# A state-space scan on one Trainium2 core: delta and delta*u spread over the states by DMA instead of by matmul

## The reference, cut to what matters

```python
u = silu(xc + conv_b)
dt, Bm, Cm = split(einsum('gld,ed->gle', u, x_proj_w), [1, 17])
delta = softplus(einsum('glr,dr->gld', dt, dt_proj_w) + dt_proj_b)
A = -exp(A_log)
def step(h, inputs):
    d_t, u_t, B_t, C_t = inputs
    dA = exp(d_t[..., None] * A)
    h = h * dA + (d_t * u_t)[..., None] * B_t[:, None, :]
    return h, einsum('gdn,gn->gd', h, C_t)
y = (ys + u * D) * silu(z)
```

## Time and profile before

| | us |
|---|---|
| median of 3 runs | 10411.63 (10410.5 to 10415.53) |
| the profiled execution, as timed | 10411.98 |
| its span | 10410.2 |
| of it the Mamba stage, first `drive` to last gate | 709.89 to 8072.94 |
| mean granted clock of TensorE, share of full speed | 0.878 |

### The profile page before, as it was taken

How to read it: one execution, slowest core, us unless ns; L and a number is a source line. 1 busy time by engine, 2 the same in 40 slices (tenths; PEclk the granted TensorE clock), 3 DMA queues, 4 the chain that set the end, 5 groups by cost and what they waited for, 6 DMA issues and landing times. The chain is left out here.

```text
span 10410.2 us, 140735 instructions
## 1 busy us (share of the span) xinstructions
PE 8332.9 (80%) x34187; PEld 4314.8 (41%) x34187; DVE 7595.6 (73%) x10036; ACT 5478.6 (53%) x9098; POOL 5384.7 (52%) x4490
## 2 busy tenths in 40 slices
PE   9977777777777777777777777777777899999997
PEld 9942222222222222222222222222222599977996
DVE  7769898898989898898989889898988112211222
ACT  0346666666666666666666666666666013311332
POOL 0027677777777777676777777677777000000000
PEclk9978888878888888888888788888888999999998
DMA  9631111111111111111111111111111100030002
GB/s 175 170 80 33 32 35 30 38 28 35 32 32 35 29 36 28 38 29 35 33 31 36 28 36 31 33 32 32 35 30 36 56 10 0 0 75 19 0 0 49
DMA packets 644678, 403.37 MB, mean 39 GB/s; under 512 B 399312, under 2 KB 631120, under 8 KB 643664
## 3 DMA queue, kind: packets, MB, share of 16 engines
q1 hardware_dynamic: 407888, 318.19, 12.2%
q10 hardware_dynamic: 236032, 77.08, 3.2%
HBM read 136.43 MB, written 103.80 MB: 23 GB/s over the span
## 5 line engine op out<-in xcount | busy, mean ns | idle before, releaser
L636 POOL TENSOR_TENSOR prod<-hs,bsp 128x448 f32<-128x448 f32 x3584 | 4378.9, 1248 | 1489.7 <-PE ps L647 800.0
L624 DVE TENSOR_TENSOR_SCAN hs<-da,hs,ps 128x448 f32<-128x448 f32 x3072 | 3482.8, 1134 | 1.5
L605 ACT ACTIVATE da<-ps,nega 128x448 f32<-128x448 f32 x3586 | 2215.2, 634 | 1746.5 <-PE ps L588 1698.8
L597 PE MATMUL ps<-stack,seld 96*128 96x448 bf16 x3586 | 1438.1, 401 | 1643.0 <-DVE hs L624 1603.6
L615 DVE TENSOR_TENSOR ps<-ps,bsp 128x448 f32<-128x448 f32 x3585 | 2190.3, 611 | 658.3 <-PE ps L597 634.7
L597 PEld LDWEIGHTS ps<-stack,seld 96*128 96x128 bf16 x3586 | 357.7, 100 | 3442.7 <-DVE hs L624 2917.5
L887 PE MATMUL ps<-pv,ws 128*128 128x224 f32 x8800 | 1692.3, 354 | 9.4 <-ACT pv L1040 7.1
L887 PEld LDWEIGHTS ps<-pv,ws 128*128 128x128 f32 x8800 | 1656.8, 188 | 45.5 <-issue 7.8
L588 PE MATMUL ps<-stack,seld 96*128 96x448 bf16 x3587 | 1428.4, 398 | 177.3 <-ACT da L605 177.3
L1221 DVE SCALAR_TENSOR_TENSOR pv<-ps,R 128x224 f32<-128x224 f32 x880 | 422.1, 480 | 1279.4 <-PE ps L887 1279.4
L647 PE MATMUL ps<-prod,wc 128*32 128x448 f32 x7200 | 1039.0, 655 | 0.0
(11 more groups left out here) (120 smaller groups left out, 8203.5 us busy)
## 6 DMA issues: line engine op xcount, KB each, us to landing
stack<-parts SPq DMA_DIRECT2D x2700, 56.0 KB, 2.0
lnx<-in_x SPq DMA_DIRECT2D x118, 224.0 KB, 2.5
lny<-y_nchw SPq DMA_DIRECT2D x118, 224.0 KB, 2.7
x_column_pairs<-otile SPq DMA_DIRECT2D x225, 116.0 KB, 1.7
xpad<-x_column_pairs SPq DMA_DIRECT2D x32, 812.0 KB, 4.3
xpad<-in_x SPq DMA_DIRECT2D x64, 392.0 KB, 6.8
y_pairs<-yout ACTq DMA_DIRECT2D x32, 784.0 KB, 6.9
yin<-y_pairs SPq DMA_DIRECT2D x32, 784.0 KB, 4.3
```

Source lines behind the costliest of these rows:

```text
L597: pe.matmul(ps[:, du_bank(st, j), 0:T], seld[0:96, b, :], stack[:, st.t % 2, 1, grp, :], start=True, stop=True).then_inc(S["du_spread"], 1)
L605: a.activation(da[:, j % 8, :], ps[:, D_BANK + j % 2, 0:T], ACT.Exp, scale=nega[:, j:j + 1])\
L624: v.tensor_tensor_scan(hs[:, j, :], da[:, j % 8, :], ps[:, du_bank(st, j), 0:T], 0.0 if first else hs[:, j, T - 1:T], ALU.mult, ALU.add)\
L636: g.tensor_tensor(prod[:, j % 8, :], hs[:, j, :], bsp[:, st.t % 2, 1, :], ALU.mult)\
```

## The change

The spreads by matmul go, and with them the bf16 parts: `cast_part`, `rest_of`, `stack_parts`, `seld`, `stack`, and the two PSUM regions that they wrote. Instead, SP stores the delta tile (delta and delta*u side by side, 128 x 896) to one of two DRAM buffers, waits until it has landed, and then issues one load per unit that reads 8 of its 128 rows sixteen times, once for each state, into one of 8 slots of `spread`, 128 x 896. A load for unit n waits until scan n-8 is done, which frees the slot. Eight of the loads of a tile are issued in the tile before, behind the store. `decay` reads delta from the slot and `drive` reads delta*u from it.

B goes from its matmul (`b_states`, a PSUM bank of its own for each parity) straight to `drive`, which multiplies the slot by the bank and writes one of three PSUM banks; C is still copied to SBUF, now as `csp`. `decay` runs four units ahead of `scan` instead of two. The constant matrices are laid out in another order of rows (states outermost), which changes no sizes but the removed `select_d`.

```diff
-PE_AT = {0: ["bc0", "last3"], 3: ["bc1"], 5: ["project", "lnc"], 8: ["sum0", "lnv"], 10: ["tap0", "tap2"],
+PE_AT = {0: ["last3"], 1: ["b"], 3: ["bc1"], 5: ["project", "lnc"], 8: ["sum0", "lnv"], 10: ["tap0", "tap2"],
-DVE_AT = {0: ["add_x"], 3: ["min", "gate"], 6: ["rest0"], 8: ["rest1"], 10: ["scale"]}
+DVE_AT = {0: ["add_x"], 3: ["min", "gate"], 10: ["scale"]}
-LEAD = {"du": 2, "delta": 3, "decay": 2, "drive": 1}
+LEAD = {"decay": 4, "drive": 1}
+SLOTS = 8
+    copies = nc.dram_tensor("delta_and_du", (2, P, 2, T), F32, kind="Internal").ap()
+            spread = sb(m, "spread", [P, SLOTS, 2, T])
+            csp = sb(m, "csp", [P, 2, T])
...
-                g.wait_ge(S["split"], st.next)
+                g.wait_ge(S["dlt_stored"], st.next * 16)
...
-        def cast_part(a, st, part):
-        def rest_of(v, st, part):
-        def stack_parts(sp, st):
+        def b_states(pe, st):
+
+            pe.wait_ge(S["u_ready"], st.next + 1)
             if not st.ahead:
+                pe.wait_ge(S["dbu_done"], st.tile * UN + 2)
+            pe.matmul(ps[:, B_BANK + st.par, 0:T], wcs("spread_bc", 0, P), u[:, st.next_u, :], start=True, stop=True)\
+                .then_inc(S["b_ready"], 1)
+
+        def store_delta(sp, st):
+
+            sp.wait_ge(S["delta_u"], st.next + 1)
+            sp.dma_start(copies[st.par], dlt[:, :, :]).then_inc(S["dlt_stored"], 16)
+            sp.wait_ge(S["dlt_stored"], st.next * 16 + 16)
+            sp.sem_inc(S["gates"], 1)
+
+        def load_spread(sp, tile, par, j):
+
+            b, grp = j // GR, j % GR
+            n = tile * UN + j
+            sp.wait_ge(S["scan_done"], n + 1)
+            lo = DI * grp + 8 * b
+            src = copies[par, lo:lo + 8].rearrange("r a t -> r (a t)").partition_broadcast(NS)
+            sp.dma_start(spread[:, j % SLOTS, :, :], src).then_inc(spread_in[j % SLOTS], 16)
...
+        def decay(a, st, j):
+
+            n = st.tile * UN + j
+            wait_spread(a, st, j)
+            a.wait_ge(S["scan_done"], n + 1)
+            a.activation(da[:, j % 8, :], spread[:, j % SLOTS, 0, :], ACT.Exp, scale=nega[:, j:j + 1])\
+                .then_inc(S["exp_done"], 1)
+
+        def drive(v, st, j):
+
+            wait_spread(v, st, j)
             if j == 0:
+                v.wait_ge(S["b_ready"], st.tile + 1)
+            v.wait_ge(S["scan_done"], st.tile * UN + (j + 9 - dbu_bank_back(st, j)))
+            v.tensor_tensor(ps[:, dbu_bank(st, j), 0:T], spread[:, j % SLOTS, 1, :], ps[:, B_BANK + st.t % 2, 0:T],
+                            ALU.mult).then_inc(S["dbu_done"], 1)
...
                     if st.has_ln:
                         ln_load(sp, st)
-                    stack_parts(sp, st)
-                    store(sp, tile, par, img, k)
+                    for j in range(SLOTS, UN):
+                        load_spread(sp, st.tile, t % 2, j)
+                        if j == 13:
+                            store(sp, tile, par, img, k)
+                    store_delta(sp, st)
+                    for j in range(SLOTS):
+                        load_spread(sp, st.next, st.par, j)
...
                     for j in range(UN):
-                        spread_du(pe, *unit(st, j + LEAD["du"]))
-                        spread_delta(pe, *unit(st, j + LEAD["delta"]))
```

148 lines of the change are left out of this document (45 added, 103 removed).

## The result

| | before | after |
|---|---|---|
| median, us | 10411.06 (10403.75 to 10415.53) | 11397.59 (11393.64 to 11421.56) |
| ratio to before | 1 | 1.0953 (95%: 1.0934 to 1.0972) |
| profiled span, us | 10410.2 | 11391.9 |
| one tile of the Mamba stage, us | 32.87 | 32.87 + (11391.9 - 10410.2) / 224 = 37.25 |

The kernel became 9.5% slower, where 9500 us were forecast. The time lies 198 us above the forecast's range, which ended at 11,200.

What follows compares the result with a forecast made beforehand. VectorE was taken to bound the kernel at 32.87 us a tile; a serial store-load-engine cycle of 28.8 us would replace this, saving 912 us over 224 tiles: 10412 - 912 = 9500 us, 8-in-10 range 9250 to 11,200.

Steps and rivals of the forecast that it cites:

- The price of a load: Spread loads on the DMA queue: 1.43 us of data time each at 320 GB/s, just within VectorE's beat of 1.57.
- Its own rival: Loads slower than VectorE's beat, since sixteen parts read the same DRAM rows; 11,200 us at 240 GB/s; chance 0.30.
- the point of decision: Load rate of 268 GB/s, at which DMA alone takes today's 32.87 us a tile; below it the kernel is slower.
- Step 1: SP, from the end of scan 7: issues load 15, then the delta store, 0.375 us per issue, 0.5 us reached.
- Step 2: Delta store lands: 2.5 us, plus 1.0 for the data of load 15 ahead of it, so 4.0 us reached.
- the far bound of 6: Upper end given for the delta store's time, 6 us, by a median of 6.9 us; the lower end was 2.5.
- Step 3: Next tile's first loads: load 16 out at 4.1 us, landing in 3.25, two more at 1.43 each; load 18 at 10.2.
- Steps 4 to 6: ScalarE from decay 18 through dq (to 18.5 us), GpSimd's ds2 and ds1 (2.34), VectorE from delta_min through scan 7 (7.44): 28.4.
- Step 5: GpSimd's ds2 and ds1 after ScalarE's dq: 2.34 us, reaching 20.95 us.
- The cycle: From scan 7 through store, loads, ScalarE, GpSimd and VectorE to the next tile's scan 7: 28.8 us, ending last; chance 0.50.
- the rival's signs: Slow loads would show as drive and decay waiting every unit, landing over 6 us, DMA share 0.9 or more, under 250 GB/s.
- The estimate from the Trainium skill: Store and loads at 2.0 us fixed plus bytes over 436 GB/s: cycle 28.0 us, about 9330 us in all.

Runs made afterwards that it cites:

- e0: Changed kernel with streams of 24 loads ahead of its Mamba stage: 8 rows sixteen times took 49.0 us, 128 neighbouring rows 31.1.
- e5: Changed kernel with other load streams ahead of its Mamba stage: one row 128 times 30.5 us, 2 rows 64 times 31.0, 4 rows 32 times 30.6.
- e8: Changed kernel, each load reading 32 rows four times (outermost count 32, wrong channels): 10629.66 us, ratio 1.0216.
- e1: Changed kernel, each load reading the 128 different rows of the delta tile instead of 8 rows sixteen times (wrong channels): 10475.57 us, ratio 1.0065.
- e7: Changed kernel with delta store issued behind load 12 and layer-norm loads behind load 10 of the tile before: 10463.62 us, ratio 1.0051.
- e9: Changed kernel with loads of 32 rows four times (wrong channels), delta store behind load 12 and layer-norm loads behind load 10: 9624.57 us, ratio 0.925.
- h3: Whole kernel on the changed one's idea, units of 32 rows times 4 states, delta store and layer-norm loads issued earlier: 9631.9 us, ratio 0.9258.
- e2: Changed kernel with the delta store issued behind load 12 instead of load 15: 10889.24 us, ratio 1.0461; its queue case expected 10,950, its chain case 10,600.
- e6: Changed kernel with layer-norm loads issued behind load 10 of the tile before, for 6 of 7 such tiles: 11081.94 us, ratio 1.0641.

## Why the prediction was wrong, point by point

- **The price of a load failed.** This is the term that gave the wrong sign. It stood at 1.43 us, from a line through two packet sizes, 320 GB/s. The trace has 1.96 in the stream, and 245 GB/s at full share. The prediction treated the packet's length as all that sets a rate. The order in which rows are dealt sets it as well: the same bytes in the same packets take 0.64 of the time (31.25 of 49.0 us) when the outermost count is 32. Its own rival named the right wall and 268 GB/s as the point of decision. But it blamed the shared source, which e0 and e5 exclude in the stream and e8 as the main cause in the loop.
- **A moved step was not counted.** Step 1 says what stands on SP's queue around the store, and nothing of `ln_load` at the head of the tile. That head is now reached only behind load 7 of the tile, which waits for scan 15 of the tile before. VectorE wants the data at once, at `add_x` behind unit 0. Before, SP issued these loads right behind the output store, with the queue idle: in one tile `lny` at 4267.44 and `add_x` at 4282.69, 15 us later. This is the 964 us of waits. Putting 6 of 7 of them earlier is worth 316 us alone; the likely reason that it is no more is that the slow loads then set the end (share 0.94 against 0.89).
- **Step 2, the store, was too small.** 3.5 us were given from its issue to its landing, and SP was to issue load 16 4.1 us after the end of scan 7. That scan ended at 4523.24 in the tile shown (it started at 4522.10), and load 16 went out at 4532.16, 8.9 us later. The store landed in 6.6 us in the median: of the loads ahead of it on the queue not one but four had yet to land in the tile shown. The prediction's sign for a wrong step 2 was "over 6 us". Even with fast loads it lands in 5.6 to 5.8 (e1, e8), close to the far bound of 6 that the step gave.
- **Even the right rate would not have saved the sign.** e1 and e8 load in orders that reach 342 and 341 GB/s at full share in the loop, above the 320 assumed, and are still 0.65% and 2.2% slower than before. Nor do the places alone: e7 is 0.5% slower. Both had to be mended (e9, h3) for the gain.
- **Step 3** had 6.1 us from the first load's issue to load 18. In the next tile's trace load 16 was there 4.7 us after the issue at 4532.16 (`drive` starts at 4536.87) and the third one at 4540.68, after 8.5 us.
- **Steps 4 to 6 held in their durations.** From the table load to the end of dq 7.64 us, forecast 7.65. `drive` 613 ns, forecast 611. `decay` of unit 16 waits 5.45, forecast 5 to 7. `delta_min` waits for ds1, the right releaser, but for 4.56 us, not 1.5 to 3. Step 5 has a slip: 18.5 and 2.34 are 20.84, not 20.95, so the cycle should have read 28.7 us and the forecast about 25 us less.
- **The cycle was the wrong thing to end last.** 28.8 plus 4.8 for the store (8.9 - 4.1) and 2.4 for the loads (8.5 - 6.1) gives 36.0, and the tile shown, one without layer norm, took 35.8 (from unit 16's `decay` at 4501.09 to the `drive` of its successor at 4536.87). But the first added term is time behind other loads on the queue and the second the slower loads themselves, and the queue was full from the first load to the store. So the bytes over the rate plus the hole behind the store set the end, as the rival said, and e2 agrees: 35.0 us, near its queue case. The cycle itself shows where the loads are fast, in e1: 31.1 us for a tile without layer norm.
- **The break-even and the rival.** At 240 GB/s the rival gave 36.4 us per tile and 11,200; it took 37.25 and 11,398. The mechanism was sized well; the ln loads, 1.4 us a tile by e6, more than cover the missing 0.85. The rival had a chance of 0.30, and that it came true doesn't by itself make the chance wrong; but the fit behind the 320 GB/s rested on no transfer of this shape. Of the rival's signs landing over 6 us (7.1), a share of 0.9 and less than 250 GB/s (0.89 and 218) came. "`drive` and `decay` wait in every unit" was met in part: `decay` waited 2203 times in 3584 units, `drive` only 287 us in all.
- **The estimate from the Trainium skill** was further off. "DMA: Bandwidth & Descriptors", section "Anatomy of one DMA", gave 9330 us with 436 GB/s; here the nearest rates show only with an outermost count of 32 or more, 407 to 410 GB/s in the table. And its section "Rules for kernel authors" advises an outermost count that is a multiple of 16, so that all 16 engines are used: in these runs all 16 are, but 16 gives 235 to 254 GB/s and 32 gives 408, so for the rate the measurement decides.

## What to carry to other kernels

When a stage that was bound by an engine is moved onto the DMA queues, price the load by a stream of exactly its access pattern, not by its bytes; and write out the whole issuing order of the queue, with everything that others need from it, since each wait in it delays all that stands behind. Where data must be repeated over partitions, measure the orders in which it can be read and choose the layout for a fast one: here 32 rows times 4 states instead of 8 times 16, together with the two moves on the queue, turned 9.5% slower into 7.4% faster; the moves alone came to 0.5% slower.

## What the runs showed of the hardware that was not expected

- A 128-partition load of 448 KB streams at 235 to 254 GB/s with an outermost count of 16, at about 400 with 32, 64 or 128. In both all 16 engines show as busy, so the DMA share doesn't tell a slow pattern from a fast one; GB/s at full share does. The cause is open.
- An outermost count of 24 (96 partitions, share 0.7) is slow too, 186 GB/s.
- One row read 128 times at once costs nothing against 128 different rows, 30.5 and 31.1 us for 24 loads.
- An outermost count of 8 uses half of the engines (share 0.5), and then 8 rows each 16 times run at 207 GB/s, while 16 rows walked through 8 times run at 124.
- A store of 448 KB landed in 2.9 us in the median with two in flight and nothing else on the queue (e0_rates), and in 6.6 behind the loads of the changed kernel.
